# Batch 0's second-layer weights summed by VectorE, batch 1's by GpSimd, in a four-layer fp32 kernel on one core

## What is computed

```
x = x + sum over the top 2 of 8 skills of w * mlp0(x, skill) + mlp0(x, shared)     # gelu(x @ gate) * (x @ up) @ down, 1024 wide
x = x + (silu(x @ W_up[e].T + b_up) * (x @ W_gate[e].T + b_gate)) @ W_down[e].T + b_down   # e = argmax(cond_8[b]), 512 wide
x = x + x @ (sum over g of cond_8[b, g] * weight[g] * mask).T + bias
x = x + x @ W_base.T + b_base + 2 * sum over e of cond_8[b, e] * (x @ As[e].T) @ Bs[e].T
```

## Time and profile before

| | |
|---|---|
| median of 3 runs | 489.08 us |
| the profiled execution | 489.0 us, its span 487.3 us, granted TensorE clock 1.00 |
| TensorE (PE) busy | 477.1 us, 98% of the span, 2166 matmuls |
| weight loads (PEld) | 393.7 us, 81% |
| VectorE (DVE) busy | 399.8 us, 82% |
| ScalarE (ACT) busy | 274.2 us, 56% |
| GpSimd (POOL) busy | 71.1 us, 15% |
| DMA | 47.33 MB, mean 97 GB/s |

### The profile page before, as it was taken

One profiled execution on the slowest core, in us unless ns is written; L12 is line 12 of the kernel. 1 busy time (PEld: TensorE's weight loads), 2 busy tenths in 40 slices (PEclk: granted clock), 3 DMA queues, 4 the chain that ended last, 5 costly groups with the idle time before them and its releaser, 6 DMA issues.

```text
span 487.3 us, 6862 instructions
## 1 busy us (share of the span) xinstructions
PE 477.1 (98%) x2166; PEld 393.7 (81%) x2166; DVE 399.8 (82%) x690; ACT 274.2 (56%) x448; POOL 71.1 (15%) x88
## 2 busy tenths in 40 slices
PE   9999988999999999999999999999999999999997
PEld 7887857668888888888888888888888888888886
DVE  7889979999877589698997979898887799974455
ACT  5557546557635474456646656676766356554432
POOL 0913279940001000200000020000000100000000
DMA  5988773403822138432382035304049323000002
GB/s 164 215 238 247 99 149 118 130 0 87 195 66 66 44 95 171 123 109 65 112 143 70 1 92 146 108 24 127 3 98 187 106 65 110 21 1 1 0 1 86
DMA packets 112908, 47.33 MB, mean 97 GB/s; under 512 B 66457, under 2 KB 111641, under 8 KB 112873
## 3 DMA queue, kind: packets, MB, share of 16 engines
q1 hardware_dynamic: 109728, 41.30, 34.4%
q0 software_dynamic: 2560, 5.21, 4.5%
q10 hardware_dynamic: 584, 0.39, 0.3%
HBM read 44.79 MB, written 2.10 MB: 96 GB/s over the span
## 4 chain that ended last, share of the span: by engine, by line
PE 78%; SPq 8%; DVE 7%; issue 2%; DMA 2%; ACT 1%; DVEq 0%; ACTq 0%
PE bank_a L1690 6%; PE bank_a L1691 6%; PE bank_a L1692 6%; PE bank_b L1690 6%; PE bank_b L1692 6%; PE bank_b L1691 6%; SPq L512 4%; PE tail L1714 4%; PE tail L1715 4%; PE tail L1718 4%; PE out L1718 3%; PE out L1714 3%; PE out L1715 3%; DMA raw<-in_L_cond_skill_down 2%; PE bank_a L1957 2%
## 5 line engine op out<-in xcount | busy, mean ns | idle before, releaser
L731 ACT ACTIVATE hid_hi<-hid 128x512 fp32r<-128x512 f32 x84 | 53.0, 631 | 84.1 <-DVE hid L1024 53.5
L1032 DVE TENSOR_TENSOR hid_lo<-hid,hid_hi 128x512 fp32r<-128x512 f32 x84 | 57.6, 686 | 18.4 <-ACT hid_hi L731 18.4
L1024 DVE SCALAR_TENSOR_TENSOR hid<-bank_b,mine,hid 128x512 f32<-128x512 f32 x64 | 47.4, 740 | 19.4 <-PE bank_b L1692 18.4
L723 ACT ACTIVATE hid<-bank_a 128x512 f32<-128x512 f32 x68 | 40.3, 593 | 37.7 <-PE bank_a L1692 36.5
L1013 DVE TENSOR_TENSOR res_lo<-raw,res_hi 128x768 fp32r<-128x768 f32 x36 | 35.2, 978 | 2.3 <-ACT res_hi L710 2.3
L710 ACT ACTIVATE res_hi<-raw 128x768 fp32r<-128x768 f32 x36 | 30.2, 840 | 3.0 <-DMA raw<-in_L_cond_skill_down 2.9
L1013 DVE TENSOR_TENSOR w_lo<-raw,w_hi 128x768 fp32r<-128x768 f32 x30 | 28.5, 950 | 1.7 <-ACT w_hi L710 1.7
L1690 PE MATMUL bank_a<-x_hi,res_hi 128*128 128x512 f32 x74 | 28.9, 390 | 0.0
L1691 PE MATMUL bank_a<-x_lo,res_hi 128*128 128x512 f32 x74 | 28.8, 390 | 0.0
L1692 PE MATMUL bank_a<-x_hi,res_lo 128*128 128x512 f32 x74 | 28.8, 389 | 0.0
L1690 PE MATMUL bank_b<-x_hi,res_hi 128*128 128x512 f32 x74 | 28.8, 389 | 0.0
(11 more groups left out here) (362 smaller groups left out, 1344.8 us busy)
## 6 DMA issues: line engine op xcount, KB each, us to landing
raw<-in_L_cond_skill_down SPq DMA_DIRECT2D x64, 128.0 KB, 3.3
raw<-in_L_cond_skill_gate SPq DMA_DIRECT2D x31, 256.0 KB, 3.1
raw<-in_L_cond_skill_up SPq DMA_DIRECT2D x31, 256.0 KB, 3.4
raw<-in_L_cond_shared_down SPq DMA_DIRECT2D x18, 128.0 KB, 3.9
...
```

Of the source, the lines that this page charges most:

```text
L723: nc.scalar.activation(hid[:, tile_of(g)], bank_a[tile_of(g)][:, :], func, **kw).then_inc(act_ready, 1)
L731: nc.scalar.activation(hid_hi[:, tile_of(g)], hid[:, tile_of(g)], ACT.Copy).then_inc(hid_hi_ready, 1)
L1024: ins = nc.vector.scalar_tensor_tensor(tile, bank, weight, tile, ALU.mult, ALU.mult)
L1032: nc.vector.tensor_tensor(hid_lo[:, tile], hid[:, tile], hid_hi[:, tile].bitcast(F32), ALU.subtract).then_inc(hid_lo_ready, 1)
```

## The change

Four things move, and the arithmetic stays as it is.

1. `a2` of batch 0 is summed by VectorE in batch 1's chunks 0 to 4 and beside layer `l1` (`A_FIRST`, `A_BESIDE_FIRST`), and split beside `l1`'s chunk 2. `a2` of batch 1, until now VectorE's at chunks 6 to 12 (`A_SECOND`), is summed by GpSimd, in `second_a2`, which waits until batch 0's is split (`weights_lo` 2) and stands ahead of the store of batch 0. GpSimd's bias DMAs now come before the sum.
2. The joint pieces of batch 0 from the second on are loaded ahead of their neighbours, and the three `first_l1` loads are spread: one after the first joint piece (0, 2), two after (0, 4). The loads of `x` 2 and 3 move from after piece (1, 2) to after (1, 6).
3. The turning of `l1`'s chunks goes from units 1, 2, 3, 4 to units 1, 3, 5 and batch 1's chunk 1 (low parts at units 2 and 4, and chunks 0 and 3). `bias_lora` goes from chunk 3 to chunk 1.
4. `c_product` of batch 0 goes from after chunk 8's `down` to between chunk 10's gate and up and chunk 9's `down`.

```diff
-C_PLACE = {0: 9, 1: 11, 2: 1, 3: 3}
+C_PLACE = {0: 10, 1: 11, 2: 1, 3: 3}
 CA_PLACE = {6: 0, 14: 1}
...
 CA_LO_AT = {8: 0, 17: 1}
-A_SPLIT_AT = {1: 0, 13: 1}
-A_SECOND = {6: (0,), 7: (1, 2), 8: (3, 4), 9: (5, 6), 10: (7,), 11: (8,), 12: (9,)}
+A_FIRST = {1: (0, 1, 2), 3: (3, 4)}
+A_BESIDE_FIRST = {0: (5, 6, 7), 1: (8, 9)}
+A_SECOND_SPLIT = 13
 OUT_PLACE = {1: 9, 2: 7}
...
 BIAS_BASE_AT = 1
-BIAS_LORA_AT = 3
+BIAS_LORA_AT = 1
 BIAS_AT = 3
+TURN_REST_LO_AT = {0: 2, 3: 3}
+TURN_REST_AT = 1
 L1_TURN = {13: 0, 14: 1, 15: 2, 16: 3}
...
 XSUM_PLACE = 12
-PAIR_TURN = {0: {1: 0, 2: 1, 3: 2, 4: 3}, 2: {1: 0, 2: 1, 4: 2, 6: 3}}
-PAIR_TURN_AT = {0: {2: 0, 3: 1, 4: 2, 5: 3}, 2: {2: 0, 3: 1, 5: 2, 7: 3}}
+PAIR_TURN = {0: {1: 0, 3: 1, 5: 2}, 2: {1: 0, 2: 1, 4: 2, 6: 3}}
+PAIR_TURN_AT = {0: {2: 0, 4: 1}, 2: {2: 0, 3: 1, 5: 2, 7: 3}}
 REST_TURN = {4: 0, 6: 1, 8: 2, 10: 3}
...
-PIECE_ORDER = ([("own", 0, c) for c in range(0, 10, 2)] + [("joint", 0, 2), ("own", 0, 10), ("own", 0, 12), ("joint", 0, 4), ("own", 0, 14),
+PIECE_ORDER = ([("own", 0, c) for c in range(0, 12, 2)] + [("joint", 0, 2), ("own", 0, 12), ("joint", 0, 4), ("own", 0, 14),
                 ("joint", 0, 6), ("own", 0, 16)]
...
                     load_x(1)
-                if (kind, b, c) == ("own", 0, 12):
-                    for n in range(3):
-                        first_l1(n)
-                if (kind, b, c) == ("own", 1, 2):
+                if (kind, b, c) == ("joint", 0, 2):
+                    first_l1(0)
+                if (kind, b, c) == ("joint", 0, 4):
+                    first_l1(1)
+                    first_l1(2)
+                if (kind, b, c) == ("own", 1, 6):
                     sp.wait_ge(turn_f, 3 * C1)
...
-            def first_a2():
+            def second_a2():
...
                 pool.wait_ge(tail_free, len(PREPS))
-                nc.gpsimd.tensor_scalar(a2[:, :], w2_raw[:, 0, :], picks[:, 0, 5:6], None, ALU.mult).then_inc(a2_step, 1)
+                pool.wait_ge(weights_lo, 2)
+                nc.gpsimd.tensor_scalar(a2[:, :], w2_raw[:, 0, :], picks[:, 1, 5:6], None, ALU.mult).then_inc(a2_step, 1)
                 for n in range(1, E):
...
                         part = slice(k * D, (k + 1) * D)
-                        pool.wait_ge(a2_step, n)
+                        pool.wait_ge(a2_step, A_STEPS + n)
                         wait(pool, a2_sum, n - 1 + k)
-                        nc.gpsimd.tensor_scalar(share, w2_raw[:, n, part], picks[:, 0, 5 + n:6 + n], None, ALU.mult).then_inc(a2_share, 1)
+                        nc.gpsimd.tensor_scalar(share, w2_raw[:, n, part], picks[:, 1, 5 + n:6 + n], None, ALU.mult).then_inc(a2_share, 1)
                         pool.wait_ge(a2_share, KD * (n - 1) + k + 1)
                         nc.gpsimd.tensor_tensor(a2[:, part], a2[:, part], share, ALU.add).then_inc((a2_sum, a2_step)[k], 1)
-                pool.wait_ge(a2_step, E)
+                pool.wait_ge(a2_step, A_STEPS + E)
                 nc.gpsimd.tensor_tensor(a2[:, :], a2[:, :], mask_nat[:, :], ALU.mult).then_inc(a2_step, 1)
-                pool.wait_ge(a2_step, E + 1)
+                pool.wait_ge(a2_step, A_STEPS + E + 1)
                 for k in range(KD):
...
             pool.dma_start(bias_all[:, 3, 0:P], u3_dram.broadcast_to([P, P])).then_inc(u3_in, 16)
-            first_a2()
             pool.wait_ge(bias_cols_ready, 1)
...
             for b in range(1, B):
+                if b == 1:
+                    second_a2()
                 if b <= JOINT:
...
                     if b == 1 and c == 2:
+                        weights_split_hi(a2_hi, a2[:, :], (a2_step, A_STEPS))
                         later_x_hi(2)
...
                     hidden_hi(b, n)
+                    if i in TURN_REST_LO_AT:
+                        turn_chunk_hi(0, TURN_REST_LO_AT[i])
                     if i == X1_PLACE:
...
                         weights_split_hi(c3_hi, c3[:, :], (weights_f, b + 1))
-                    if i in A_SPLIT_AT:
-                        weights_split_hi(a2_hi, a2[:, :], (a2_step, A_STEPS * (A_SPLIT_AT[i] + 1)))
+                    if i == A_SECOND_SPLIT:
+                        weights_split_hi(a2_hi, a2[:, :], (a2_step, A_STEPS * (b + 1)))
                     if i in L1_TURN_LO:
...
+                for n_step in A_BESIDE_FIRST.get(c, ()):
+                    a2_step_n(0, n_step)
                 if c == 1:
...
                 elif c == 2:
+                    weights_split_lo(0, 2, a2_hi, a2_lo, a2[:, :])
                     later_x_lo(2)
...
                         x_sum(0)
+                    if i in TURN_REST_LO_AT:
+                        turn_chunk_lo(0, TURN_REST_LO_AT[i])
+                    if i == TURN_REST_AT:
+                        turn_chunk(0, C1 - 1)
                     if i == X1_PLACE:
                         x1(b)
+                    for step_n in A_FIRST.get(i, ()):
+                        a2_step_n(0, step_n)
                     if i == L1_PLACE[b]:
...
                         weights_split_lo(b, 1, c3_hi, c3_lo, c3[:, :])
-                    if i in A_SPLIT_AT:
-                        weights_split_lo(A_SPLIT_AT[i], 2, a2_hi, a2_lo, a2[:, :])
-                    for step_n in A_SECOND.get(i, ()):
-                        a2_step_n(b, step_n)
+                    if i == A_SECOND_SPLIT:
+                        weights_split_lo(b, 2, a2_hi, a2_lo, a2[:, :])
                     if i == XSUM_SECOND:
...
                     l0_gate_up(0, i)
+                    if i == C_PLACE[0]:
+                        c_product(0)
                     if i:
                         l0_down(0, i - 1)
-                    if i == C_PLACE[0]:
-                        c_product(0)
```

## The result

| | before | changed |
|---|---|---|
| median | 489.59 us (488.16 to 490.37) | 486.14 us (485.32 to 487.03, 4 runs) |
| the profiled execution, its span | 489.0, 487.3 us | 487.03, 485.3 us |
| TensorE busy | 477.1 us | 477.9 us |
| VectorE, ScalarE, GpSimd busy | 399.8, 274.2, 71.1 us | 395.6, 272.5, 71.0 us |

The ratio is 0.9933, 95% interval [0.9907, 0.9959]: 3.4 us, 0.7% faster. The prediction said 484.8, in a range of 482.2 to 488.2; it was 1.3 us too low.

The account below looks back on a forecast made before the run. TensorE, busy 477.1 of 487.3 us, was taken as the bound, so only its standing still could be won: 489.0 - 7.4 + 0.9 + 2.25 = 484.8 us, range 482.2 to 488.2 with the rivals.

Parts of the forecast that it names:

- gross gain: TensorE's stops before c_product and in the joint units, with their restarts, all go: 0.6 + 2.8 + 4.0 = 7.4 us.
- Joint piece (0, 4): Joint units: issued ahead of W_down, over 13 us earlier, so the 2.68 us wait with its restart goes: 2.8 us.
- GpSimd out of the stretch and turning spread out: Joint units: shorter L1556 and moved turning end the waits at unit 1's start and in units 3 and 4: 4.0 us.
- c_product: Batch 0: behind twelve other matmuls its operand is no longer late; the wait goes with its restart, taken as 0.6 us.
- Piece (0, 14): Behind W_up, 2.3 us late for TensorE at worst, nothing if SP's queue is freed sooner; taken as 0.9 us lost.
- VectorE in batch 1: Added sum steps and turning delay (1, 2), (1, 3), (1, 4) and l1: 2.25 us lost, 0.2 of it at (1, 2).
- Rival A: VectorE's batch 1 work hides in idle time, 5.6 us beside l1, and (0, 14) is in time: 481.6 us; chance 0.17.
- Hidden, at no cost: GpSimd's batch 1 sum slows VectorE by 7.7 us, covered by 6.7 us idle and 6.8 us got back: nothing lost.
- Rival B: The wait moves from joint piece (0, 4) to (0, 14), early W_gate sharing the DMAs: 487.6 us; chance 0.15.
- Rival E: Beside GpSimd's batch 1 sum fourteen VectorE instructions wait 1.4 us each, 6.2 us lost: 491.0 us; chance 0.03.

Follow-up runs that it names:

- loads_only: The kernel before with only the new order of loads: 487.69 us, ratio 0.9961.
- loads_back: The changed kernel with the old order of loads (joint piece (0, 4) again behind the second pair of W_down loads): 488.32 us, ratio 0.9985.
- turn_back: The changed kernel with the turning back in joint units 1 to 4 and the loads of x 2 and 3 behind piece (1, 2): 483.33 us, ratio 0.9874.
- c_back: The changed kernel with c_product back behind the down products of chunk 8: 485.79 us, ratio 0.9942.
- turn_back_wgate: turn_back with the W_gate loads issued behind joint piece (0, 4) and not behind (0, 2): 485.16 us, ratio 0.993.
- fit_idle: The changed kernel with four of VectorE's five first sum steps moved: two ahead of chunk 1's low hidden part, two behind hidden tile 4: 482.98 us, ratio 0.9866.
- after_short_gpsimd: The changed kernel with GpSimd's sum for batch 1 cut to 8 columns of each half from the second product on: 485.83 us, ratio 0.993.
- turn_back_w2: turn_back with GpSimd's load of the second-layer weights after chunk 14's low part and not chunk 8's: 481.88 us, ratio 0.9855.
- fit_idle_w2: fit_idle with the late load of the second-layer weights of turn_back_w2: 482.01 us, ratio 0.9838.
- before_short_gpsimd: The kernel before with GpSimd's sum for batch 0 cut to 8 columns of each half from the second product on: 485.16 us, ratio 0.9905.
- sum_back: The changed kernel with batch 0's second-layer sum back on GpSimd in the joint units and batch 1's on VectorE: 483.65 us, ratio 0.9896.

## Why the prediction was right, and what it had wrong

**The gross gain (7.4 us, less 0.9 for piece (0, 14)): right in the sum.** From 45 to 111 us the table has 9.2 us of lost starts before and 2.0 after, 7.2 us, of which the forecast's net was 6.5. Term by term it was less tidy:
- *Joint piece (0, 4), 2.8:* the wait goes and comes back as the loads do, with 3.3 us in the trace of loads_only and 4.7 in that of loads_back. By the medians it is worth less, 1.2 and 2.2 us, so the size stands for the profiled executions only. The term left out that such a stop can bring the slow clock with it, 1.6 us more; that the profile of before had none of it was chance (29 of 59 of its runs had it).
- *GpSimd out of the stretch and turning spread out, 4.0 together:* the sum was right (5.1 us lost in the joint units of loads_only, 0.9 in the change), the split wrong. The prediction wanted both. turn_back has no wait in the joint units with the turning where it was; the first edit alone is enough. Since the second then has nothing to win, its cost in batch 1 is a pure loss.
- *c_product, 0.6:* the wait goes, and in the traces no more than 0.2 us of its gain arrives (1.1 us lost from 45 to 62 us against c_back's 1.3), since TensorE meets VectorE again ten us later. The times are too close to tell.
- *Piece (0, 14), 0.9:* nothing was lost, but not by the case that the prediction named. SP's queue was free not sooner but 2.0 us later than forecast (69.52 for 67.5), as `W_up` held it for 7.8 us. The piece was in time because TensorE was late: it had lost 4.8 us before 62 us, against 2.1 in before. That is luck; in turn_back_wgate, with 1.0 us lost, a piece issued at 69.15 made it wait 1.4 and 1.7 us.

**VectorE in batch 1 (2.25 us): right in place and size.** 1.9 us are lost from 142 to 160 us, at chunks (1, 3), (1, 4) and the start of `l1`; that (1, 2) would lose 0.2 was wrong. Rival A's ground, idle time beside `l1`, did not help, for the reason given: the five first steps stood ahead of it. What the prediction did not see is that idle time stood ahead of them too, 1.08 us behind the split of chunk 1, where fit_idle puts two of them, as it puts the other two into the 1.29 us behind (1, 4).

**"Hidden, at no cost", GpSimd in 173 to 213 us: wrong by 0.8 us.** The 7.7 us against 13.5 us of room was a sum over 40 us; two instructions of VectorE just ahead (L1023, 1.12 us in place of 0.95, at 172.97, and L1042, 1.22 in place of 0.69, at 174.01) were enough to be late for `ca_product` at 176.69. after_short_gpsimd takes that wait away. fit_idle has the same lengthened instructions at the same times and no wait, since TensorE comes there at 176.7 and not at 176.2: the contention costs only what the margin does not cover.

**What made it slower than forecast was mostly in no term.** The terms above, as measured, give 489.0 - 7.2 + 1.9 + 0.8 = 484.5 us, level with the forecast; the median was 486.14, the profiled execution 487.03. *Own piece (0, 12)* was not in the sum, though it is within the 7.2: the early `W_gate` and GpSimd's load of the second-layer weights fill the DMA engines when it comes. 0.8 us in the profiled run, over 3 us in two others, nothing where the load is later (turn_back_w2, fit_idle_w2). Rival B had named the shared DMAs, but for another piece. *The head (5 to 45 us)* loses 1.3 us in the profile of before and 3.7 after. The change's first moved load there is own piece (0, 10), at 26.70 us in SP's queue in place of 31.53, but the load that comes late was issued ahead of it: ScalarE's wait for the piece that it splits near 27 us is 1.89 us in before and 4.06 in the changed kernel. Over all kernels, with the old order of loads or the new, waits of 0.8 to 2.2 us go with 1.0 to 1.7 us lost in the head, and waits of 2.8 to 4.1 us with 2.2 to 3.7 (before_short_gpsimd is an exception, 0.95 and 2.9). The head lost 2.2 us or more in all eight kernels whose profiled execution was the slowest of their runs, and 1.7 or less in five of the other six. So this varies from run to run, and a median holds less of it than the change's profile; that VectorE, busy without a gap from 29.7 to 45 us in the trace of before, hands a late start on from chunk to chunk is my reading, which no run tested.

So the change gives 7.2 us, and takes back 2.7 in batch 1 (1.9 and 0.8) and in its profile 2.4 in the head: 2.1, where the profiled executions differ by 2.0. The medians differ by 3.4, which leaves 1.1 us for the head and what else varies; that the head's share is chance is the likeliest reading and not shown, as each kernel was profiled once. turn_back, fit_idle and sum_back show that the 2.7 was not needed.

VectorE's instructions with two SBUF inputs were lengthened beside GpSimd in all kernels with a full sum on it, and L1551 and its like, which read PSUM, in none (0.69 us at most). This is the rule of the Trainium skill's page "SBUF — State Buffer" (section "Who interferes with whom"). The same section of the Trainium skill says that the order of issue decides who is blocked. The trace agrees for the adds: the 46 instructions that started during one ended 0.55 us after it. Beside multiplications it may be GpSimd that waits (L642 of the changed kernel takes 0.92 to 2.15 us), which no run separates. The prediction's price, 0.55 us for each L1556, was read where that instruction happened to start with the add, and is close to the most that one can lose to an add of 0.74 us (0.74 + 0.55 - 0.68 = 0.61); to read the price off one line was luck. Rival E took the multiplications' 1.4 us for the lock, where it is the adds after which VectorE's long instructions end.
